# A four-layer graph network on one core: the first tile's products in another order, half of the first weights' low parts on POOL, and the cells named earlier

## What is computed

```python
h = relu(layernorm(x)); x = x + L0(h)   # x1 = h @ W1 + b1 (1024 -> 512); four gated graph convolutions with tanh
h = relu(layernorm(x)); x = x + L1(h)   # h @ W.T + bias, W = zeros(1024, 1024).at[row, col].add(edge_weight)
h = relu(layernorm(x)); x = x + L2(h)   # graph convolution with self loops, symmetric norm, relu
h = relu(layernorm(x)); x = x + L3(h)   # graph attention: exp(-leaky_relu(al[src] + ar[dst])), normalised, elu
```

## Time and profile before

| | |
|---|---|
| median of three runs | 989.35 us (988.47 to 989.62) |
| the profiled execution | 988.97 us, span 987.5 us |
| PE busy | 969.5 us, 98% of the span |
| DVE busy | 674.9 us, 68% |
| ACT busy | 444.7 us, 45% |
| POOL busy | 137.5 us, 14% |
| granted clock of PE, mean | 0.998 |

### The profile page before, as it was taken

One profiled execution on the slowest core, in us unless ns is written; L12 is line 12 of the kernel. 1 busy time (PEld: TensorE's weight loads), 2 busy tenths in 40 slices (PEclk: granted clock), 3 DMA queues, 4 the chain that ended last, 5 costly groups with the idle time before them and its releaser, 6 DMA issues.

```text
span 987.5 us, 14131 instructions
## 1 busy us (share of the span) xinstructions
PE 969.5 (98%) x5199; PEld 807.1 (82%) x5200; DVE 674.9 (68%) x1225; ACT 444.7 (45%) x664; POOL 137.5 (14%) x191
## 2 busy tenths in 40 slices
PE   5999999999999999999999999999999999999998
PEld 4788878888888888888888888888888888888887
DVE  7887797788788779468884115333336664988887
ACT  5688874554554557223335446001012222455444
POOL 3022510000000001222331000010000000333231
PEclk9999999999999999999999999999999999999999
DMA  7256490000000005543421040732231130201222
GB/s 254 89 189 228 123 274 1 0 23 0 0 21 0 0 0 117 98 148 127 133 101 65 1 172 6 276 123 107 86 128 70 69 122 1 87 17 69 85 85 81
DMA packets 26005, 88.28 MB, mean 89 GB/s; under 512 B 3384, under 2 KB 3580, under 8 KB 25808
## 3 DMA queue, kind: packets, MB, share of 16 engines
q1 hardware_dynamic: 15072, 52.82, 15.0%
q0 software_dynamic: 10880, 34.74, 11.6%
HBM read 59.23 MB, written 33.56 MB: 94 GB/s over the span
## 4 chain that ended last, share of the span: by engine, by line
PE 93%; DVE 4%; ACT 1%; issue 1%; DMA 1%; POOL 1%; another core or an unknown queue 0%; SPq 0%; DVEq 0%; ACTq 0%; POOLq 0%
PE ps L613 22%; PE ps L2222 12%; PE ps L2196 11%; PE ps L2116 9%; PE ps L2118 9%; PE ps L2117 9%; PE ps L2172 5%; PE ps L2168 5%; PE ps L596 2%; PE ps L2039 1%; PE ps L2041 1%; PE ps L2040 1%; PE ps L1966 1%; PE ps L2010 1%; PE ps L1969 1%; PE ps L2233 1%
## 5 line engine op out<-in xcount | busy, mean ns | idle before, releaser
L2116 PE MATMUL ps<-g_hi,mask_hi 128*128 128x512 f32 x400 | 157.8, 395 | 0.9 <-DVE mask_lo L1581 0.9
L2118 PE MATMUL ps<-g_hi,mask_lo 128*128 128x512 f32 x400 | 156.1, 390 | 0.0
L2117 PE MATMUL ps<-g_lo,mask_hi 128*128 128x512 f32 x400 | 155.9, 390 | 0.0
L1118 ACT ACTIVATE mask<-ps,v 128x640 f32<-128x640 f32 x80 | 63.1, 793 | 95.5 <-PE ps L2118 49.0
L2222 PE MATMUL ps<-y_all,att_hi 128*128 128x512 f32 x380 | 103.7, 393 | 0.3 <-DVE att_lo L1830 0.3
L2116 PEld LDWEIGHTS ps<-g_hi,mask_hi 128*128 128x128 f32 x400 | 75.1, 188 | 19.7 <-DVE mask_lo L1581 2.3
L2118 PEld LDWEIGHTS ps<-g_hi,mask_lo 128*128 128x128 f32 x400 | 75.1, 188 | 15.9
L2117 PEld LDWEIGHTS ps<-g_lo,mask_hi 128*128 128x128 f32 x400 | 75.2, 188 | 14.9
L613 PE MATMUL ps<-w,hT_hi 128*128 128x512 f32 x320 | 86.6, 393 | 0.0
L579 ACT ACTIVATE hT_hi<-ps 128x1024 fp32r<-128x1024 f32 x30 | 30.8, 1026 | 123.2 <-PE ps L596 123.0
L2222 PEld LDWEIGHTS ps<-y_all,att_hi 128*128 128x128 f32 x380 | 70.5, 188 | 15.0 <-issue 0.7
(11 more groups left out here) (227 smaller groups left out, 1951.3 us busy)
## 6 DMA issues: line engine op xcount, KB each, us to landing
xin<-x_after SPq DMA_DIRECT2D x20, 512.0 KB, 3.3
xres<-x_after POOLq DMA_DIRECT2D x20, 512.0 KB, 3.6
x_after<-xres POOLq DMA_DIRECT2D x20, 512.0 KB, 2.9
w_raw<-in_L_gnn_W SPq DMA_DIRECT2D x8, 1024.0 KB, 10.6
x_after<-g POOLq DMA_DIRECT2D x20, 256.0 KB, 7.5
xin<-in_x SPq DMA_DIRECT2D x9, 512.0 KB, 3.4
x_after<-in_x SPq DMA_DIRECT2D x8, 512.0 KB, 5.0
weight_rows<-weight_row POOLq DMA_DIRECT2D x8, 512.0 KB, 4.0
```

What stands on the lines that cost most here:

```text
L1118: nc.scalar.activation(mask[k][:, :], U_ALL, ACT.Tanh, bias=v[:, s:s + 1]).then_inc(tanh_ready, 1)
L2116: nc.tensor.matmul(SUMS[dd], mask_hi[k][:, cols], g_hi[:, s, :], start=(s == 0), stop=False)
L2117: nc.tensor.matmul(SUMS[dd], mask_hi[k][:, cols], g_lo[:, s, :], start=False, stop=False)
L2118: last = nc.tensor.matmul(SUMS[dd], mask_lo[k][:, cols], g_hi[:, s, :], start=False, stop=(s == T - 1))
```

## The change

PE: `pick_edges` is cut into `pick_ends` and `pick_parts`. After the ends, the new `x1_first` transposes tile 1, then makes tile 0's products by weight part: for each slice high x high and low x high, with `pick_parts` in the middle, and after them the eight products with the weights' low parts. DVE makes four of those low parts, POOL the other four behind its splitting of the edge weights. DVE's blend of the ends, tile 1's low part and the naming of the cells move ahead of the loop, and so ahead of tile 2's statistics. ACT copies the picked ends and takes tile 1's high part in the middle of its casts. Tile 1's bank is opened after POOL's low parts are done.

```diff
+POOL_LOWS = 4
+    def lows(layers):
+        return KT * layers - POOL_LOWS
...
# POOL, behind the splitting of the edge weights
+        for k in range(KT - POOL_LOWS, KT):
+            pool.wait_ge(w_hi_ready, k + 1)
+            nc.gpsimd.tensor_tensor(w1_lo[:, k, :], w1_raw[:, k, :], w1_hi[:, k, :].bitcast(F32),
+                                    ALU.subtract).then_inc(parts_chain, 1)
...
# ACT
         for k in range(KT):
             if k == 2:
                 place_bias(0)
+            if k == KT // 2:
+                act.wait_ge(ends_picked, 2)
+                for n in range(2):
+                    nc.scalar.activation(edges[0:EP, n, :], PICKED[n][0:EP, 1, :], ACT.Copy).then_inc(picked_copied, 1)
+                transposed_act(act, d, 0, 1)
             if k % 2 == 0:
                 act.wait_ge(w_landed[k // 2], 16)
             nc.scalar.activation(w1_hi[:, k, :], w1_raw[:, k, :], ACT.Copy).then_inc(w_hi_ready, 1)
-        act.wait_ge(ends_picked, 2)
-        for n in range(2):
-            nc.scalar.activation(edges[0:EP, n, :], PICKED[n][0:EP, 1, :], ACT.Copy).then_inc(picked_copied, 1)
         act.wait_ge(parts_picked, 3)
...
         for t in range(T):
-            if t + 1 < T:
+            if 0 < t < T - 1:
                 transposed_act(act, d, (t + 1) // 2, (t + 1) % 2)
...
# DVE
-        for k in range(KT):
+        for k in range(KT - POOL_LOWS):
             dve.wait_ge(w_hi_ready, k + 1)
             nc.vector.tensor_tensor(w1_lo[:, k, :], w1_raw[:, k, :], w1_hi[:, k, :].bitcast(F32),
                                     ALU.subtract).then_inc(w_lo_ready, 1)
+        blend_ends()
+        transposed_dve(dve, d0, 0, 1)
+        name_cells()
         for t in range(T):
             place_dve(t, 0)
...
-            if t == 0:
-                blend_ends()
-            if t + 1 < T:
+            if 0 < t < T - 1:
                 transposed_dve(dve, d0, (t + 1) // 2, (t + 1) % 2)
             if t == 0:
-                name_cells()
                 blend_parts()
...
# PE
             if t == 1:
+                pe.wait_ge(parts_chain, 5 + POOL_LOWS)
                 pe.wait_ge(blend_chain, 3)
                 open_bank(1)
...
+        def x1_first():
+
+            transpose_pe(pe, d0, 0, 1)
+            pe.wait_ge(bias_placed, 1)
+            for k in range(KT):
+                if k == KT // 2:
+                    pick_parts()
+                pe.wait_ge(w_hi_ready, k + 1)
+                nc.tensor.matmul(PRODUCT0[0], hT_hi[0][:, k, :], w1_hi[:, k, :], start=False, stop=False, skip_group_check=True)
+                nc.tensor.matmul(PRODUCT0[0], hT_lo[0][:, k, :], w1_hi[:, k, :], start=False, stop=False, skip_group_check=True)
+            for k in range(KT):
+                if k < KT - POOL_LOWS:
+                    pe.wait_ge(w_lo_ready, k + 1)
+                else:
+                    pe.wait_ge(parts_chain, 5 + k - (KT - POOL_LOWS) + 1)
+                last = nc.tensor.matmul(PRODUCT0[0], hT_hi[0][:, k, :], w1_lo[:, k, :], start=False, stop=(k == KT - 1), skip_group_check=True)
+            last.then_inc(product_ready[0], 1)
+
         open_bank(0)
         transpose_pe(pe, d0, 0, 0)
         sum_rows_below()
-        pick_edges()
-        for t in range(T):
+        pick_ends()
+        x1_first()
+        for t in range(1, T):
```

More of the change, by code:

```diff
@@ L608, in product_pe @@
             if first:
-                pe.wait_ge(w_lo_ready, KT * d.n + k + 1)
+                pe.wait_ge(w_lo_ready, lows(d.n) + k + 1)
             for left, rights in ((hT_hi[b], (hi, lo)), (hT_lo[b], (hi,))):
@@ L785, in _ @@
         load_x3(1)
-        sp.wait_ge(w_lo_ready, KT * 4)
+        sp.wait_ge(w_lo_ready, lows(4))
         with sp.Fori(2, HT) as i:
@@ L1934, in pick, with pick_ends @@
             return last
-        def pick_edges():
+        def pick_ends():
             pe.wait_ge(picks_ready, 2 * EDGE_TILES)
@@ L1942, in pick_edges, with pick_parts @@
                 pick(PICKED[n], lambda t: of[0:EDGE_ROWS, t, :]).then_inc(ends_picked, 1)
+        def pick_parts():
             pe.wait_ge(parts_chain, 5)
@@ L2036, in x1_pe @@
                     spread_u(0, 0)
-                if t == 0:
-                    pe.wait_ge(w_lo_ready, k + 1)
                 nc.tensor.matmul(PRODUCT0[b], hT_hi[b][:, k, :], w1_hi[:, k, :], start=False, stop=False, skip_group_check=True)
@@ L2191, in gcn_product @@
                 if t == 0:
-                    pe.wait_ge(w_lo_ready, KT * 2 + k + 1)
+                    pe.wait_ge(w_lo_ready, lows(2) + k + 1)
                 for part, rights in ((0, (W_HI[2], W_LO[2])), (1, (W_HI[2],))):
```

## The result

The changed kernel took 990.6 us (median of 20 executions, 989.89 to 991.53), the kernel before 989.08 us (20 executions beside it, 988.33 to 990.10). The ratio is 1.0017, interval 1.0011 to 1.0023: 1.5 us slower, less than the 2.0 us that were set as the bound, so "same" by it, with a sign that is certain. The forecast was 991.2 us. The profiled execution has a span of 989.1 us, before 987.5.

The account below looks back on a forecast made before the run. PE work was taken to bound the kernel, with DVE's chain over ACT setting its wait at 42.33. Terms -2.7 +5.3 -4.2 +3.8 +1.35 -1.7 make +1.85 us: median 991.2 us, range 986.9 to 993.0.

Parts of the forecast that it names:

- PE's order, tile 0: PE, head: tile 1's transposes follow the end picks at 13.4, filling a 1.95 us stall; products end 22.9 to 24.5.
- Statistics put behind the naming: DVE, head: 5.3 us of blend, low part and naming now stand ahead of tile 2's statistics.
- S: Start of tile 2's statistics on DVE: 18.66 before, forecast 21.3 without turns and 25.1 with them.
- Turns between POOL and DVE: DVE's naming beside POOL's low parts: three POOL operations come in between in turn, +3.8 us.
- Slack of the chain: From tile 2's statistics to cell group 0: 7.65 us needed where 11.87 passed before, -4.2 us.
- Half rate at tile 1: PE idles some 5 us before tile 2's transposes; clock halves for 4.0 us, +1.35 us at the cells.
- The fall at 43.85 that goes: PE's wait before cell group 3 shrinks from 1.74 to some 0.7 us; the clock drop behind it vanishes, -1.7 us.
- The sum: Whole kernel: all terms together make +1.85 us, median 991.2 us.
- POOL hidden: Rival, chance 0.22: naming and POOL's low parts pass one another, cells 1.6 us earlier, 987.8 or 986.1 us.
- PE bound by POOL: Rival, chance 0.05: DVE keeps its turn, POOL's low parts wait, last low product at 25; 989.0 us.
- The clock giving nothing back: Rival, chance 0.13: clock falls at tile 1 and again at a later wait; 992.9 to 993.4 us.

Follow-up runs that it names:

- e3: Changed kernel with tile 2's statistics ahead of the naming of the cells on DVE; 988.03 us, 0.9987 of the kernel before.
- e5: e3 with all eight low parts of the first weights on DVE, none on POOL; 988.45 us, 0.9994 of the kernel before.
- e1: Changed kernel with all eight low parts on DVE again, none on POOL; 991.04 us, 1.0021 of the kernel before.
- e2: e1 plus four useless 128x512 subtractions on POOL beside DVE's naming; 995.81 us, 1.0066 of the kernel before.
- e9: Changed kernel unaltered, run once more for another profiled execution; 990.09 us.
- e4: Changed kernel with sixteen more matmuls of zeros on PE ahead of opening tile 1's bank; 989.25 us, 1.0004 of the kernel before.
- e11: Kernel before unaltered, run once more for another profiled execution; 988.10 us.
- e8: Changed kernel with POOL's four low parts held back until the naming is nearly through; 989.15 us, 0.9996 of the kernel before.
- e10: Changed kernel with ACT taking cell group 2 before the relu of tile 4; 989.68 us, 1.0008 of the kernel before.
- e6: e3 with ACT taking cell group 2 before the relu of tile 4; 984.22 us, 0.9944 of the kernel before.
- e7: Kernel before with only ACT's taking of cell group 2 moved before tile 4's relu; 986.32 us, 0.9965.

## Why the prediction was right

- **PE's order, tile 0.** Transposes of tile 1 forecast for 13.4, measured 13.8, in an execution whose first tile landed 0.25 us later. Tile 0 through at 23.9, forecast 22.9 to 24.5. Right, and worth nothing in this kernel, where PE then stands 4.05 us (forecast some 5). The new order on PE was never run alone.
- **Statistics put behind the naming.** S forecast at 25.1, measured 24.84. e3 and, without POOL's part in it, e5 against e1 show this order to be the cause: with it mended the time falls by 2.6 us in both (3.0 and 2.7 by the ratios). That S came so near is in part luck: the naming began at 18.77 and not at 18.2, and its turns cost 0.8 us less than forecast.
- **Turns between POOL and DVE.** Forecast by the earlier trace rows, seen as three long operations, raised to four by e2 and removed by e1. The size was off: +3.0 us for three turns (+3.3 in e9) and not +3.8, since a short DVE operation adds next to nothing to POOL's turn. POOL's own price was right (1.31 us, forecast 1.29). By the Trainium skill (SBUF — State Buffer, "Who interferes with whom") the second to issue waits in full; the traces agree (in e2 1.53 us for an operation of 0.41 that stood behind POOL's).
- **Slack of the chain.** Relu 1.86 us after S, transposes 3.06, tile 2's low part 6.44 after it: forecast 1.85, 3.05 and 6.45.
- **Half rate at tile 1.** Forecast +1.35 us by 4.0 us at half rate, cells at 34.1; the half rate lasted 3.4 us, and the cells were at 33.58, of which the half rate is 1.1 us by the trace (judging at 33.50, tile 2's low part done at 32.4). e4 has 1.35 us in the time.
- **The fall at 43.85 that goes.** Wait forecast at 0.7 us, measured 0.95; the fall is gone in both profiled executions of the changed kernel. The term was mis-sized twice. It is worth 1.4 us and not 1.7, by 4.6 against 3.2 us; and it was taken as a property of the kernel before, though it belongs to that one execution: of 63 timed executions of that kernel 36 have a mean clock of 0.999 or more (median 988.49 us), 27 have less (989.42). So in the median only part of it comes back.
- **The sum.** Forecast +3.55 at the cells and -1.7 at the fall, +1.85; the first pair of profiles has +3.05 and -1.4, +1.65; the pair e11 and e9 has +1.9 and nothing back; the medians of 20 differ by 1.5. Both terms of the forecast were read from one execution of the kernel before, in which the cells were early and the clock fell, and the two lean opposite ways. That their sum fits the median so well is luck; the mechanism behind the loss (order, turns, late relu, half rate) is not. The exact share of each in the median stays open.
- **The rivals.** POOL hidden: out, by e1 and e2. PE bound by POOL: not so here, but it is what e8 makes of it. The clock giving nothing back: 7 of the 20 executions of the changed kernel have a mean clock of 0.996 and lie at 991.1 to 991.5, 13 have more and lie at 989.9 to 990.9. The one execution with a longer half rate in a profile (e10, mean clock 0.997) has a longer stretch at tile 1 and no second one; that the 7 are the same was not seen in a profile of the changed kernel itself. Not run: each part of the change alone in the kernel before.

## What to carry to other kernels

Work that is moved to POOL to relieve DVE can come back in full as waiting: here 2.7 us of low parts went to POOL and three turns of 1.0 us came back, because DVE's operations beside it read SBUF twice or were short casts and scalar forms. Operations that read PSUM and the statistics kept their time beside POOL's low parts (1.21 us for tile 1's low part at 17.65 in the changed kernel, 1.29 for the statistics at 19.11 in e3); POOL's work belongs beside such. When a block of work is pulled forward on an in-order engine, ask what it now stands in front of; here it was the statistics that release the next tile's relu, and they were worth more than all that was pulled forward. And a wait that the profile puts down to one engine may be another's: here it was one call moved on ACT, worth 3.1 us.

## What was not expected of the hardware

- The same kernel with the same wait of 1.74 or 1.75 us has the clock fall behind it in one execution and not in the next, and a wait of 2.52 us did it in e3 and not in the profiled execution of e5. It goes with sets of times 0.9 to 1.4 us apart: cleanly in e3 (986.6 to 986.8 with the mean clock at 1.0, 988.0 to 988.6 with 0.998), only in the median in the kernel before, where executions at 1.0 reach 990.97 us. So the clock is not the whole scatter: with the wait gone, five executions lie within 0.3 us in e6 but within 1.4 in e7. Why the clock falls in one execution and not in the next stays open.
- In the head the granted clock of the windows reads 1.00 while the products cost 0.43 us each (15.90 to 18.46 in the changed kernel, 0.23 from 20.28 on). The clock that the profile shows does not account for every slow stretch; here only the distance of the starts told it.
- In the turns the short DVE operations pay and POOL hardly does: its four low parts take 5.23 us beside the naming and 5.21 in e2, against 5.08 in e3, where one turn was left. It is not immune. In e8 its first low part started at 20.32, just behind a DVE operation of 0.68 us (20.28), took 1.78 us where the median of the four is 1.27, and the four took 5.48. In e11 a cast of POOL in the splitting (L852) took 1.58 us beside DVE's low parts, where it took 0.73 in the first profile: this is part of why PE picked later there.
